# Four of the curve's twelve lines taken off TensorE in the feed-forward stage of a graph layer

## The reference, cut to what matters

```python
x = x + gnn(layernorm(x), edges) + linear_attention(layernorm(x))
h = round_to_1_256th(layernorm(x) @ w1 + b1)          # 3125 x 512
y = interp(h, 33 points of the exact GELU on [-4, 4])  # 0 below -4, h above 4
y = round_to_1_256th(y)
out = x + round_to_1_256th(y @ w2 + b2)                # 3125 x 1024
```

## Time and profile before

| what | us |
|---|---|
| median of three runs | 3107.56 (3103.63 to 3111.19) |
| the profiled execution, its own time | 3111.14 |
| its span, first to last instruction | 3109.0 |
| granted PE clock, mean | 0.994 |
| feed-forward stage, about | 2706 to 3109 |

### The profile page before, as it was taken

The page is one execution under the profiler, slowest core; times in us unless marked ns, Lnnn a source line. Parts: engine busy times, 40 slices in busy tenths (PEclk is TensorE's granted clock), DMA queues, the critical chain, the costliest instruction groups (busy, mean ns, idle before and its releaser), DMA issues. The chain is left out here.

```text
span 3109.0 us, 41236 instructions
## 1 busy us (share of the span) xinstructions
PE 3037.5 (98%) x14012; PEld 2500.3 (80%) x14012; DVE 2604.5 (84%) x4513; ACT 1164.5 (37%) x1499; POOL 803.3 (26%) x716
## 2 busy tenths in 40 slices
PE   8999999989999999899999999999999999999998
PEld 6888888867888888677778888888888888878887
DVE  6777777767777777698989999999999988788886
ACT  3111111122111111233346566556656644565554
POOL 1256666754655666200000000000000000000000
PEclk9999999999999999999999999999999999999999
DMA  9943333353444444555655356447446634233331
GB/s 341 374 99 65 60 60 60 73 134 71 84 93 93 80 93 93 159 167 170 184 165 161 112 154 167 128 127 202 123 121 168 168 93 118 75 88 106 104 106 53
DMA packets 184432, 395.83 MB, mean 127 GB/s; under 512 B 78181, under 2 KB 79061, under 8 KB 184310
## 3 DMA queue, kind: packets, MB, share of 16 engines
q1 hardware_dynamic: 106230, 308.58, 33.6%
q0 software_dynamic: 71440, 65.24, 11.4%
q10 hardware_dynamic: 6640, 20.45, 2.0%
HBM read 303.36 MB, written 90.81 MB: 127 GB/s over the span
## 5 line engine op out<-in xcount | busy, mean ns | idle before, releaser
L1580 PE MATMUL G_acc<-values,whole_plain 125*125 125x257 f32 x5000 | 1095.9, 381 | 15.8 <-DVE whole_plain L1524 8.6
L1580 PEld LDWEIGHTS G_acc<-values,whole_plain 125*125 125x125 f32 x5000 | 935.4, 188 | 166.0 <-DVE whole_plain L1524 11.8
L375 POOL DMA_INDIRECT counts<-E_twins_now,E_cells_now x392 | 672.9, 1717 | 308.6 <-DMA counts<-E_twins_now,E_cells_now 171.3
L1424 ACT ACTIVATE whole_plain<-whole_plain,G_asrc_slope 125x750 f32<-125x750 f32 (+1 forms) x400 | 377.6, 945 | 388.3 <-DVE whole_plain L1511 387.3
L1511 DVE SCALAR_TENSOR_TENSOR whole_plain<-whole_plain,G_asrc_most 125x750 f32<-125x750 f32 (+1 forms) x400 | 409.5, 1024 | 32.8 <-PE G_acc L1580 31.7
L1396 POOL DMA_DIRECT2D gat<-xT_plain x100 | 53.7, 537 | 1027.4 <-ACT xT_plain L1440 1027.4
L268 PE MATMUL V_v_ps<-whole,xT_space 128*125 128x512 f32 x1200 | 285.1, 399 | 8.0 <-DVE xT_space L296 4.0
L268 PE MATMUL Q_mm<-Q_mixer,xT_space 128*125 128x512 f32 x1200 | 284.8, 396 | 5.5 <-DVE xT_space L296 5.5
L268 PE MATMUL K_k_ps<-whole,xT_space 128*125 128x512 f32 x1200 | 287.1, 398 | 3.2 <-PEq L494 3.2
L1052 DVE SCALAR_TENSOR_TENSOR N_least<-xT_plain,asrc_all,N_least 125x750 f32<-125x750 bf16 (+1 forms) x292 | 289.7, 992 | 0.0
L268 PE MATMUL K_v_ps<-K_wv,xT_space 128*125 128x512 f32 x1200 | 287.9, 395 | 0.0
(11 more groups left out here) (195 smaller groups left out, 3178.2 us busy)
## 6 DMA issues: line engine op xcount, KB each, us to landing
whole_plain<-counts SPq DMA_DIRECT2D x279, 328.1 KB
counts<-wo_raw POOLq DMA_DIRECT2D x50, 763.5 KB, 9.7
whole_plain<-counts SPq DMA_DIRECT2D x68, 382.8 KB
xT_whole<-xnT SPq DMA_DIRECT2D x50, 500.0 KB, 3.7
E_row<-edge_keys ACTq DMA_DIRECT2D x26, 512.0 KB, 3.8
xnT<-xT_whole SPq DMA_DIRECT2D x25, 500.0 KB, 4.3
V_xT_other<-xnT SPq DMA_DIRECT2D x25, 500.0 KB, 4.0
gat<-xT_plain POOLq DMA_DIRECT2D x100, 125.0 KB, 2.5
```

Source lines behind the costliest of these rows:

```text
L375: nc.gpsimd.indirect_dma_start(out=counts_cells, out_offset=bass.IndirectOffsetOnAxis(ap=self.cells_now[:, slot, c:c + 1], axis=0), in_=se ...
L1424: nc.scalar.activation(here, here, ACT.Exp, bias=asrc_slope[:, u % H, j:j + 1]).then_inc(exp_ready, 1)
L1580: m = nc.tensor.matmul(acc[0:T, t, 0:CW], weight[:, k % RING, t * T:(t + 1) * T], values[:, u % H, j, :], start=(j == 0), stop=(j == NT - 1))
```

## The change

What it does:
- The last four lines of the curve, whose kinks are all negative, no longer go to PE. ACT makes |kink_i| * max(size - knot_i, 0) of each (`folded`), and POOL subtracts the four, one after the other, from max(h, 0) in place. PE has 8 products of a tile in place of 12, ACT 8 terms for PE and 4 for POOL.
- ACT makes the size: |h|, then short = max(918/256 - |h|, 0), from which every line comes with scale -1 (or the kink) and another bias; and it makes max(h, 0) in place, which DVE had done on the way. So ACT has 15 instructions of 125x512 for a tile in place of 12, and DVE's two are gone.
- DVE's gelu is now a plain sum (`tensor_tensor`), and waits for POOL's last subtraction (`folded_in`) as well as for PE.
- The two instructions of a Newton step are `tensor_scalar` now: one stream from SBUF, the other factors as scalars per row. The first has two scalars per row (it had one), the second has one (it had none). This holds for both normalisations.
- PE frees `hid_ps` after the rounding of the hidden values (`hid_fixed`) and no longer after the size.
- POOL clears two semaphores of the first stage in the second, and sets one constant more.

```diff
-        chain.step(nc.vector.scalar_tensor_tensor(out=square, in0=inverse, scalar=minus_half, in1=inverse,
-                                                  op0=ALU.mult, op1=ALU.mult))
+        chain.step(nc.vector.tensor_scalar(square, inverse, minus_half, inverse, ALU.mult, ALU.mult))
         chain.settle()
-        chain.step(nc.vector.scalar_tensor_tensor(out=inverse, in0=square, scalar=1.5, in1=inverse,
-                                                  op0=ALU.add, op1=ALU.mult))
+        chain.step(nc.vector.tensor_scalar(inverse, square, 1.5, inverse, ALU.add, ALU.mult))
...
+            for spent in a["spent_by_keys"]:
+                nc.gpsimd.sem_clear(spent)
...
-    KN = len(CURVE)
+    KN, FOLDED = len(CURVE) - 4, 4
...
+    def folds(pool):
+        chain = Chain(pool, fold)
+
+        def body(g, n):
+            here = hid[:, n % 2, :]
+            for i in range(FOLDED):
+                chain.settle()
+                pool.wait_ge(folded_ready, g * (FOLDED + 1) + (i + 2))
+                taken = nc.gpsimd.tensor_tensor(here, here, folded[:, i, :], ALU.subtract)
+                if i < FOLDED - 1:
+                    chain.step(taken)
+            taken.then_inc(folded_in, 1)
+        over_tiles(pool, body, chain=chain, steps=FOLDED - 1, **TILES)
...
         def make_terms(g, n):
-            act.wait_ge(size_ready, g + 1)
+            here, lack = hid[:, n % 2, :], short[:, n % 2, :]
+            act.wait_ge(hid_fixed, g + 1)
+            nc.scalar.activation(lack, here, ACT.Abs).then_inc(size_made, 1)
+            act.wait_ge(size_made, g + 1)
+            nc.scalar.activation(lack, lack, ACT.Relu, bias=whole_from[:, :], scale=-1.0).then_inc(short_ready, 1)
+            nc.scalar.activation(here, here, ACT.Relu).then_inc(folded_ready, 1)
+            if fixed(g, 1):
+                act.wait_ge(folded_in, g)
+            act.wait_ge(short_ready, g + 1)
+            for i in range(FOLDED):
+                nc.scalar.activation(folded[:, i, :], lack, ACT.Relu, bias=knots[:, KN + i:KN + i + 1],
+                                     scale=CURVE[KN + i][1]).then_inc(folded_ready, 1)
             if fixed(g, 1):
                 act.wait_ge(bent_done, g)
             for i in range(KN):
-                nc.scalar.activation(terms[:, i, :], magnitude[:, n % 2, :], ACT.Relu, bias=knots[:, i:i + 1]).then_inc(terms_ready, 1)
+                nc.scalar.activation(terms[:, i, :], lack, ACT.Relu, bias=knots[:, i:i + 1], scale=-1.0).then_inc(terms_ready, 1)
...
             fix(here, here).then_inc(hid_fixed, 1)
-            dve.wait_ge(hid_fixed, g + 1)
-            chain.step(nc.vector.scalar_tensor_tensor(out=size, in0=here, scalar=-1.0, in1=here,
-                                                      op0=ALU.mult, op1=ALU.max))
-            chain.settle()
-            nc.vector.tensor_scalar(size, size, WHOLE_FROM / 256.0, None, ALU.min).then_inc(size_ready, 1)
...
+            dve.wait_ge(folded_in, g + 1)
             dve.wait_ge(bent_done, g + 1)
-            chain.step(nc.vector.scalar_tensor_tensor(out=gelu[:, :], in0=hid[:, n % 2, :], scalar=0.0, in1=bent_ps[:, :],
-                                                      op0=ALU.max, op1=ALU.add))
+            chain.step(nc.vector.tensor_tensor(gelu[:, :], hid[:, n % 2, :], bent_ps[:, :], ALU.add))
...
-            pe.wait_ge(size_ready, g)
+            pe.wait_ge(hid_fixed, g)
```

More of the change, by code:

```diff
@@ L584, in keys_and_values @@
     kb_ready, k_low, k_exp, k_ready, v_ready = sem("kb_ready"), sem("k_low"), sem("k_exp"), sem("k_ready"), sem("v_ready")
-    ones_set, diagonal_set = sem("ones_set"), sem("diagonal_set")
-    zero_filled = [sem(f"zero_filled{i}") for i in range(FILLS_AHEAD)]
-    link = sem("link")
+    diagonal_set, zero_filled = sem("diagonal_set"), [sem(f"zero_filled{i}") for i in range(FILLS_AHEAD)]
+    ones_set, link = sem("ones_set"), sem("link")
     with nc.Block() as block:
@@ L1607, in feed_forward_places @@
         x1=sb("x1", [T, 6, D]), xn=sb("xn", [T, D]), stats=sb("stats", [T, 2, 6]), moments=sb("moments", [T, 2]),
-        root=sb("root", [T, 5]), knots=sb("knots", [T, len(CURVE)]), kink_row=sb("kink_row", [T, len(CURVE)]),
+        root=sb("root", [T, 5]), knots=sb("knots", [T, len(CURVE)]), kink_row=sb("kink_row", [T, len(CURVE)]), whole_from=sb("whole_from", [T, 1]),
         base_in=sb("base_in", [T, D]), gat_in=sb("gat_in", [T, D]), raw=sb("raw", [128, KB, F]),
@@ L1611, in feed_forward_places @@
         b1_row=sb("b1_row", [T, F]), b2_row=sb("b2_row", [T, D]), geluT=sb("geluT", [128, 2, FB, T], F32R), fed=sb("fed", [T, D]))
[L1614 removed]
+Feed = namedtuple("Feed", ("link", "load_first", "load_next", "load_second_weights", "sync", "constants", "folds", "rows_high",
                            "first_weights_high", "scalar", "rows_statistics", "rows_normal", "make_kinks", "rows_low",
@@ L1628, in feed_forward @@
     least = a["nearest"].least[:, 2:4, :].rearrange("p u w -> p (u w)")
-    KN = len(CURVE)
+    KN, FOLDED = len(CURVE) - 4, 4
+    assert all(kink < 0.0 for _, kink in CURVE[KN:])
     terms = spent[:, 0:KN * F].rearrange("p (i f) -> p i f", i=KN)
     kinks = spent[:, KN * F:KN * (F + T)].rearrange("p (i t) -> p i t", i=KN)
+    folded = (a["whole_plain"][0:T, 0, :, :, :].rearrange("p s k n -> p (s k n)")[:, 8192 - FOLDED * F:8192]
+              .rearrange("p (i f) -> p i f", i=FOLDED))
     kinks_whole = least[:, 2 * WIDEST - KN * T:2 * WIDEST].rearrange("p (i t) -> p i t", i=KN)
-    x1, xn, stats, moments, root, knots, kink_row = (first[n] for n in ("x1", "xn", "stats", "moments", "root", "knots", "kink_row"))
+    x1, xn, stats, moments, root, knots, kink_row, whole_from = (
+        first[n] for n in ("x1", "xn", "stats", "moments", "root", "knots", "kink_row", "whole_from"))
     base_in, gat_in, raw1, xT, w1 = (first[n] for n in ("base_in", "gat_in", "raw", "xT", "w1"))
@@ L1637, in feed_forward @@
     RING = x1.shape[1]
-    hid, magnitude, gelu = work[:, 0:2, :], work[:, 2:4, :], work[:, 4, :]
+    hid, short, gelu = work[:, 0:2, :], work[:, 2:4, :], work[:, 4, :]
     hid_ps, bent_ps, gelu_tr = ps("hid_ps", [T, F]), ps("bent_ps", [T, F]), ps("gelu_tr", [128, FB, 128])
@@ L1644, in feed_forward @@
     in_loaded, xn_ready, turned, xT_high, xT_low = sem("in_loaded"), sem("xn_ready"), sem("turned"), sem("xT_high"), sem("xT_low")
-    hid_done, hid_fixed, size_ready = sem("hid_done"), sem("hid_fixed"), sem("size_ready")
-    terms_ready, bent_done = sem("terms_ready"), sem("bent_done")
+    hid_done, hid_fixed, short_ready = sem("hid_done"), sem("hid_fixed"), sem("short_ready")
+    size_made, terms_ready, bent_done = sem("size_made"), sem("terms_ready"), sem("bent_done")
+    folded_ready, folded_in, fold = sem("folded_ready"), sem("folded_in"), sem("fold")
     gelu_ready, gelu_turned, gelu_high, gelu_low = sem("gelu_ready"), sem("gelu_turned"), sem("gelu_high"), sem("gelu_low")
@@ L1811, in hidden @@
         def hidden(g, n):
-            here, size = hid[:, n % 2, :], magnitude[:, n % 2, :]
+            here = hid[:, n % 2, :]
             dve.wait_ge(hid_done, g + 1)
@@ L1850, in body @@
             low(nc, geluT[:, 1, :, :], gelu_tr[:, :, 0:T], geluT[:, 0, :, :]).then_inc(gelu_low, 1)
-        over_tiles(dve, body, chain=chain, steps=1 + LN_STEPS + 1 + 2, **TILES)
+        over_tiles(dve, body, chain=chain, steps=1 + LN_STEPS + 1 + 1, **TILES)
         dve.wait_ge(out_free, NT)
@@ L1913, in tensor @@
         feed(NT - 1)
-    return Feed(link, load_first, load_next, load_second_weights, sync, constants, rows_high, first_weights_high, scalar,
+    return Feed(link, load_first, load_next, load_second_weights, sync, constants, folds, rows_high, first_weights_high, scalar,
                 rows_statistics, rows_normal, make_kinks, rows_low, first_weights_low, vector, turn, first_products, tensor)
```

19 lines of the change are left out of this document (12 added, 7 removed).

## The result

The changed kernel takes 3090.33 us (median of 6 runs, 3087.92 to 3095.07), the kernel before 3107.61 us (6 runs, 3103.63 to 3111.19). The ratio is 0.9946, with a 95% interval from 0.9936 to 0.9956: 17.3 us, about 0.55% faster. The forecast was 3089 us.

A forecast was written before the change was run, and what follows sets the result against it. PE was taken as the bound, with DVE close behind. Rounds 20.5, start 0.5, end 0.3, less 0.3 for the first stage and 2.5 for the lag, make 18.5 us: 3107.6 to 3089 us, range 3081 to 3103.

The forecast's parts named there:

- PE: Curve products in the feed-forward rounds: eight for twelve, 0.93 us less a round, 20.5 us over 22 tiles.
- ACT: Fifteen instructions a tile plus gelu's high halves: 11.1 us of work in a round of 14.3, so hidden.
- The root: Newton steps: one more scalar per row in 8 instructions at 55 ns, 0.43 us more a normalisation.
- POOL: Four subtractions a tile: 1.2 us each, 0.2 us between, 5.6 us of work, hidden by some 7 us.
- Both meetings: Lock in a round: POOL's first subtraction waits for L1767; L204 waits up to 0.8 us for the fourth.
- signs of being wrong: PE waiting each round, L1767 or L204 above 1.22 and 0.81 us, subtractions of 2 us, round beyond 15 us.
- DVE as the bound: In the rounds DVE, with its wait for POOL, works 14.55 us, 0.23 more than PE's 14.32.
- the lag: DVE falls behind PE by 22 x 0.23 = 5.1 us, eats 2.5 us of slack, costs about 2.5 us.
- The two ends: Start and end of the feed-forward stage: 0.5 us gained at the start, 0.3 us at the end.
- Stages before: First stage: its first normalisation, ahead of everything, gets slower by up to 0.43 us, taken as 0.3 lost.
- no loss by the lock: POOL is short or falls between DVE's instructions: 21.0 us gained, median 3086.5; chance 0.60 together with the likeliest case.
- Slower by the lock: Rounds: from 1.5 us of lock waits all gain is lost; with 2.8 us, median 3134; chance 0.09.

The follow-up runs named there:

- the old root: The changed kernel with the root's Newton steps as before (two SBUF streams, one element): 3104.96 us, ratio 0.9988 to the kernel before.
- subtractions of 8 columns: The changed kernel with POOL's four subtractions cut to 8 of 512 columns, all waits kept: 3086.28 us, ratio 0.9925 to the kernel before.
- the root alone: The kernel before with only the root's steps changed to the new one-stream form: 3108.99 us, ratio 1.0001 to the kernel before.

## Why the prediction was right

**PE.** Eight products in place of twelve, a round of 14.32 us: measured 14.33 us, and 20.1 us over the 22 rounds where 20.5 stood.

**ACT.** Its work stays hidden. PE never waited for it in the rounds, and DVE by 0.3 us in all over the stretch of 228.6 us.

**The root.** 0.43 us forecast, from one more scalar per row in eight instructions at 55 ns each (which makes 0.44). Measured: 273 for 220 ns and 214 for 159, that is 4 x (53 + 55) = 0.43 us. What I counted as merely free of the lock is worth 14 us, as the old root showed. That this was right was luck: I had no row for one-element instructions with two streams beside a POOL tensor instruction and gave this part no price.

**POOL.** A subtraction takes 1.30 us, not 1.2, with 0.16 us between two. Both meetings came as walked through: L1801 ahead of the first (POOL waits), L203 over the fourth, 0.70 us against up to 0.8. L203's mean of 1.51 us was one of my signs of being wrong, and it came while the round stayed 14.33 us: the sign was badly chosen, since a wait of DVE only counts once DVE is the bound. The lock as the Trainium skill's SBUF — State Buffer page (section Who interferes with whom) has it, held for a whole instruction and taken by whoever comes first, agrees with the rows of POOL's subtractions above. I had written that the earlier trace rows agree too, and one of them does so only in part: L204 ended at 273.69 us, before the DMA instruction of POOL that it lay over (273.76).

**DVE as the bound: this term was wrong.** I had 14.55 us for DVE and 2.5 us lost as it fell behind by 0.23 us in each round. In fact its own work is 13.46 us and not 13.75, so with the wait it is 14.16 us, less than PE's 14.33. A later L203 would wait less for the same subtraction, so I think a lag would not have added up in this way; no run shows that. The slack that I set against the lag was wrong too: DVE has the low half of gelu 1.54 us before PE loads it (2872.87 and 2874.41 us in the changed kernel), not 2.5. The term is zero.

**The two ends: these were wrong the other way.** My 20.5 us were the curve's products of tiles 1 to 22, the measured 22 rounds hold those of tiles 2 to 23. With tiles 1 and 23 counted where the measured split has them, I had 0.5 + 0.9 = 1.4 us gained at the start and 0.9 - 0.3 = 0.6 us lost at the end, and they are 1.4 and 1.6 us lost: 2.8 and 1.0 us the wrong way. At the start my 0.5 left the lock out, though I named a price of 0 to 0.9. The timeline of the changed kernel there:

```profile
2733.39 1.36 POOL L1741 TENSOR_TENSOR F_work<-F_work,whole_plain 125x512 f32<-125x512 f32 x1 [4.59 <-ACT whole_plain L1769]
2733.51 2.32 DVE L1801 SCALAR_TENSOR_TENSOR F_x<-F_gat_in,F_base_in 125x1024 f32<-125x1024 f32 x1
...
2741.26 1.93 PE L282 MATMUL F_tr<-ident,F_xn 125*128 125x125 f32 x8 [3.53 <-DVE F_xn L203]
```

Here POOL came first and L1801 took 2.32 us in place of 1.22, and that lies on PE's path: PE waits 3.53 us for the rows of tile 3, where it waited 1.96. That is 1.1 us of the 2.8. Nearly all of the rest is the clock: from the transposes of tile 3 to the first product with the second matrix four products fewer should have made 2.79 us of 3.72, and it was 4.37. At the end the rounding of an output tile took 1.15 us in place of 0.69 beside POOL's last subtraction, but it cost next to nothing: with subtractions of 8 columns it is back at 0.69 us, and the distance between those two products with the second matrix is 10.02 us against 10.08, because then ACT's half of gelu is what DVE waits for. What was lost at the end is the clock of the last 24 products, 8.66 us for 7.42. So 0.4 us in the rounds, 2.8 at the start and 1.0 at the end went the wrong way, against 2.5 us for the lag that did not come and 0.3 for the first stage that no profile can show: these rounded terms leave 1.4 us, and the sum was off by only 1.2, 17.3 for 18.5. That is luck. The mechanism of the rounds was right; the other terms cancelled each other.

**Stages before.** The 0.3 us of the first normalisation can't be seen: the last graph product of the kernels with this root and a short gap starts anywhere from 2699.7 to 2710.6 us.

The rivals: "no loss by the lock" is right for the rounds. "Slower by the lock" did not come, but the kernel with the old root shows that little is enough to take nearly all of the gain away: two steps of the root that wait 1.0 us each, in place of L203 that waits 0.7.

## What to carry to other kernels

When work goes to GpSimd, don't ask only how long it takes there but which VectorE instructions meet it. Here those with two SBUF streams waited for the rest of one GpSimd instruction, whatever their own size, and so did large ones with one stream (L203, the roundings); each meeting must be counted so. Give the small dependent steps a form with one stream, even when it is slower by itself. Price the ends of a stage apart from its rounds: what is hidden in the steady state lay on the path of the first and the last tiles here.

## What the runs showed of the hardware

The granted clock in two stretches of each kernel: from the transposes of tile 3 into the first product with the second matrix (each stretch runs 0.17 us into it), and the last 24 products. Columns as in the earlier trace rows; the third number from the end is the clock. Before:

```profile
2739.18:2743.06 3.88, 3.88 (x21) 3.29 (x22) 3.78 (x6) 1.01 (x1) 0.00 (x0) 1.00 0.70 198
...
3096.90:3104.40 7.50, 7.42 (x24) 5.50 (x24) 1.85 (x4) 0.00 (x0) 0.00 (x0) 0.77 0.22 70
```

After:

```profile
2741.26:2745.79 4.53, 4.53 (x17) 3.95 (x18) 2.75 (x4) 2.46 (x4) 0.00 (x0) 0.62 0.76 218
...
3079.92:3088.60 8.68, 8.66 (x24) 6.41 (x24) 1.81 (x3) 0.00 (x0) 0.00 (x0) 0.65 0.23 70
```

Behind the longer wait of 3.53 us PE ran at 0.62 of its clock where it ran at full clock behind 1.96 us, and so four products fewer took 0.65 us more. Of the two levels, 0.62 means a mix with much at 1.2 GHz. The wait alone does not settle it: the second profile of before had the same slow stretch (5.29 us for 3.72) behind the same wait of 1.96 us, and behind waits of 2.40 and 2.43 us the root alone ran it in 3.72 and the kernel without a folded line in 5.31 us. The last 24 products took 5.89 us (old root), 7.16 to 7.42, or 8.35 to 8.66 us in different kernels, always behind a wait of 3.46 or 3.47 us. Here two profiles of one kernel agree: 7.42 and 7.31 us before, 8.66 and 8.57 after. So, by two profiles each, the 1.2 us at the end belong to the change, though no run shows what in it moves the clock, while at tile 3 a time can move by 1.6 us from one execution to the next. Either is as large as the error of the forecast.

A one-element instruction with one stream, 64 of each kind in the stretch above, kept its 273 and 214 ns beside POOL; the same step with two streams took 1.23 us. Among these small ones the form decides. A large instruction with one stream waits all the same (L203, 1.51 us for 0.81); what separates it from the small ones was not tested.
